# Cross-attention on one core: VectorE's mask rows, one split and one normalisation stand earlier in its order, and one set of transposes stands behind a product on TensorE

## What is computed

```python
Q = (img_embed @ Wq).reshape(B, -1, H, D).transpose(0, 2, 1, 3)
K = (sent_embed @ Wk).reshape(B, -1, H, D).transpose(0, 2, 1, 3)
V = (sent_embed @ Wv).reshape(B, -1, H, D).transpose(0, 2, 1, 3)
score = jnp.einsum('bhqd,bhkd->bhqk', Q, K) / math.sqrt(D)
score = jnp.where(mask, score, -jnp.inf)
attn = jax.nn.softmax(score, axis=-1)
ctx = jnp.einsum('bhqk,bhkd->bqhd', attn, V).reshape(B, -1, H * D)
out = ctx @ Wo + img_embed
# then layer norm over the 512 columns, times gamma, plus beta
```

## Time and profile before

| | |
|---|---|
| median of 3 runs | 364.54 us (363.69 to 364.98) |
| the profiled execution's own time | 363.32 us |
| its span, first to last instruction | 361.5 us |
| TensorE busy | 351.6 us, 97% |
| VectorE busy | 269.9 us, 75% |
| ScalarE busy | 224.4 us, 62% |
| GpSimd busy | 193.6 us, 54% |

### The profile page before, as it was taken

The page is one execution under the profiler, slowest core; times in us unless marked ns, Lnnn a source line. Parts: engine busy times, 40 slices in busy tenths (PEclk is TensorE's granted clock), DMA queues, the critical chain, the costliest instruction groups (busy, mean ns, idle before and its releaser), DMA issues. The chain is left out here.

```text
span 361.5 us, 6803 instructions
## 1 busy us (share of the span) xinstructions
PE 351.6 (97%) x2286; PEld 326.8 (90%) x2286; DVE 269.9 (75%) x504; ACT 224.4 (62%) x763; POOL 193.6 (54%) x208
## 2 busy tenths in 40 slices
PE   8999999999999899999999999999999999999993
PEld 6999999999999898899899889989988998998873
DVE  3299998773811267798897977987987988879886
ACT  2377764244334459776876776777777758767550
POOL 0045640000003856669679688688696696784234
PEclk9999999999999999999999999999999999999998
DMA  8998679866743080052241441441531422412012
GB/s 239 424 418 303 250 241 346 279 213 218 261 151 128 7 283 2 3 175 82 95 147 66 138 148 46 160 140 36 176 115 61 173 71 106 146 62 86 31 58 88
DMA packets 19682, 55.80 MB, mean 154 GB/s; under 512 B 1728, under 2 KB 3264, under 8 KB 17728
## 3 DMA queue, kind: packets, MB, share of 16 engines
q1 hardware_dynamic: 18784, 54.38, 42.2%
q10 hardware_dynamic: 864, 1.00, 1.0%
HBM read 46.98 MB, written 8.39 MB: 153 GB/s over the span
## 5 line engine op out<-in xcount | busy, mean ns | idle before, releaser
L615 PE MATMUL pair<-vw_hi,pt_hi 128*128 128x512 f32 x155 | 62.3, 402 | 0.0
L615 PE MATMUL pair<-vw_hi,pt_lo 128*128 128x512 f32 x155 | 60.8, 392 | 0.0
L615 PE MATMUL pair<-vw_lo,pt_hi 128*128 128x512 f32 x155 | 60.6, 391 | 0.0
L1182 POOL TENSOR_TENSOR out_sb<-centred,beta_sb 128x512 f32<-128x512 f32 x31 | 40.1, 1293 | 31.0 <-ACT centred L795 31.0
L750 ACT ACTIVATE prob<-c,neg_max 128x77 f32<-128x77 f32 x128 | 43.9, 346 | 0.0
L1196 POOL TENSOR_TENSOR x_sum<-xt_in 128x256 f32<-128x256 f32 x16 | 11.9, 743 | 59.5 <-DMA xt_in<-x_tiles 59.4
L1221 POOL TENSOR_TENSOR xo_lo<-x_sum,xo_hi 128x512 fp32r<-128x512 f32 x32 | 41.2, 1292 | 3.0 <-ACT xo_hi L774 3.0
L788 ACT ACTIVATE pt_hi<-pair 128x640 fp32r<-128x640 f32 x32 | 22.5, 703 | 30.4 <-PE pair L602 30.4
L1034 DVE TENSOR_TENSOR pair<-pair,x_in 128x512 f32<-128x512 f32 x31 | 21.7, 699 | 25.2 <-PE pair L615 25.1
L550 PE MATMUL pair<-a_hi,xo_hi 128*128 128x308 f32 x128 | 40.1, 313 | 0.0
L550 PE MATMUL pair<-a_lo,xo_hi 128*128 128x308 f32 x128 | 38.8, 303 | 0.0
(11 more groups left out here) (115 smaller groups left out, 958.5 us busy)
## 6 DMA issues: line engine op xcount, KB each, us to landing
w_out<-wo SPq DMA_DIRECT2D x8, 1024.0 KB, 4.8
xt_in<-x_tiles SPq DMA_DIRECT2D x16, 512.0 KB, 4.0
x_in<-x_rows SPq DMA_DIRECT2D x16, 512.0 KB, 4.8
out<-out_sb SPq DMA_DIRECT2D x31, 256.0 KB, 2.1
w_out<-wq_t SPq DMA_DIRECT2D x7, 1024.0 KB, 7.0
w_proj<-wv SPq DMA_DIRECT2D x8, 768.0 KB, 4.7
w_proj<-wk SPq DMA_DIRECT2D x6, 768.0 KB, 9.0
w_out<-wq_t SPq DMA_DIRECT2D x2, 512.0 KB, 8.2
```

Source lines behind the costliest of these rows:

```text
L615: mm = pe.matmul(ps_out[:, i % 2, 0:s.model], ps[:, j, :], v[:, b, j, :], start=(j == 0 and n == 0), stop=(j == s.key_t - 1 and n == len(p ...
L1182: pool.tensor_tensor(out_sb[i % OUT_RING][:, :], centred[i % 2][:, :], beta_sb[:, :], ALU.add)\
```

## The change

Four places in the orders of TensorE and VectorE. No instruction is added, removed or altered; only their places move (the line numbers of VectorE's instructions grow by 7, those of TensorE's later helpers by 4).

```diff
@@ TensorE: A12 becomes a helper of its own
-            def second_products(p):
+            def product_on_a(p):
 
                 b = batch_of(p)
                 pe.wait_ge(act_s1, p + 1)
                 product(p, bank_a, A12, right(a_hi, b, 1, 0), right(a_lo, b, 1, 0), False)
+
+            def second_products(p):
+
+                b = batch_of(p)
                 pe.wait_ge(act_xo_hi, SPLITS * p + 4)
@@ TensorE: pairs 0 and 1
             first_products(0)
+            product_on_a(0)
             second_products(0)
             first_products(1)
+            product_on_a(1)
             transpose_prob(0)
             second_products(1)
@@ TensorE: the loop, where the order stays as it was
                 transpose_prob(a - 1)
+                product_on_a(p)
                 second_products(p)
@@ VectorE: the last use of the first stage
                 else:
+                    if u == USES - 1:
+                        rows_for_mask()
                     split_vw(u - H)
...
-                elif u == USES - 1:
-                    rows_for_mask()
@@ VectorE: tiles 0 and 1
             residual(0)
+            split_pt(1)
             layer_norm(0)
-            split_pt(1)
@@ VectorE: the last pair
                 if p == NPAIRS - 1:
+                    normalise(a + 1)
                     split_pt(a)
-                    normalise(a + 1)
                 centre(a - 2, ps_out[:, (a - 2) % 2, 0:s.model])
```

## The result

The changed kernel takes 359.62 us (median of 4 runs, 359.38 to 359.83); the kernel before took 364.5 us in the runs beside it (363.69 to 364.98). The ratio is 0.9868 with a 95% interval of 0.9849 to 0.9887. The two profiled executions, however, stand 363.32 - 359.83 = 3.49 us apart.

What follows compares the result with a forecast made beforehand. TensorE, busy 97%, bounds the kernel, so its removed waits count: 2.1 + 0.3 + 0.5 + 0.5 = 3.4 us, off the median of 364.54 giving 361.1 us; range 359.9 to 363.2.

Steps and rivals of the forecast that it cites:

- the last line of the sum: Takes 3.4 us of removed waits off the profiled execution's time (359.9) or the median (361.1), and predicts the latter.
- Mask rows: VectorE makes them in its idle ahead of V's last split, so TensorE's bias matmul starts earlier: 2.1 us.
- The split that was overtaken: `split_vw(7)`, now behind the mask rows, still runs from 124.31 to 125.60, before transposes that come at 127.1.
- The other end, 1.9: Gain at the mask rows if VectorE is let in only when GpSimd rests: bias matmul 0.2 us late.
- Transposes behind A12: Pair 1: A12 fills TensorE's hidden wait before tile 0's transposes, saving 0.3 us.
- Split of tile 1: VectorE makes it before tile 0's layer norm, ending TensorE's stall before tile 2's transposes: counted as 0.5 us.
- the next bound: Tile 3's transposes wait for the split of tile 2, limiting the two middle places to 0.83 us together.
- The layer norm's delay: Tile 0's layer norm comes 0.74 us later, and GpSimd's work with it; GpSimd's 0.73 us idle takes it up.
- Last pair: Normalisation of tile 31 fills VectorE's idle before the split of tile 30; later waits end sooner: 0.5 us.
- the transfer: Pair 2's tiles landing late for GpSimd: gain at the mask rows eaten, 363.2 us (0.07), or slower, 365.6 (0.04).
- a new bound in the loop: Sign of being wrong: a new TensorE wait over 0.3 us, above all in pairs 0 to 3, or longer loop rounds.
- The rival of a GpSimd that holds VectorE off: Mask rows give 1.9 and the middle two places 0.5: 2.9 us in all, 361.6 us; chance 0.12.

Runs made afterwards that it cites:

- the mask rows alone: Kernel before with only the mask rows moved ahead of V's last split: 361.01 us, ratio 0.9925.
- the idle filled: Kernel before with nine matmuls on zeros run by TensorE while it waits for the unmoved mask rows: 363.18 us.
- the other three places: Changed kernel with the mask rows left where they were before: 363.2 us, ratio 0.9978 to the kernel before.
- `two_ones` early: Kernel before with only `two_ones` made ahead of V's last split, the two mask rows staying behind it: 363.03 us, ratio 0.9986.
- the transposes, the split or the last pair alone: Kernel before with one move each: tile 0's transposes behind A12, 364.49 us; tile 1's split before tile 0's layer norm, 363.69; tile 31's normalisation before tile 30's split, 363.84.

## Why the prediction was right or wrong

**The step that failed** is the last line of the sum: "Against its own time the sum gives 359.9; on the median it gives 361.1, and this is what I predict." I saw that the profiled execution was 1.2 us below the median of the runs shown and took this for an offset that the change would keep. It was no offset: the sum held every wait but left at nothing, without a reason, what may follow the longest of them, a stretch at half clock, and the change removes that too.

In these experiments the kernel before ran 69 times: 26 executions had a mean clock of 0.990 to 0.992 and a median of 364.6 us, 43 had 0.995 or more and a median of 363.3. The profiled one was of the larger group; of the three runs behind the 364.54, 364.54 and 364.98 fit the other group by their time, and 363.69 fits this one; their clocks are not known. Without the idle at the mask rows no execution was below 0.995: 10 of the changed kernel, 6 with the mask rows alone, 12 with the idle filled. With an idle of 1.8 to 2.0 us, 40 of 96 were: 26 of 69 before, 7 of 12 with the other three places, 4 of 12 with `two_ones` early, and the three executions with the transposes, the split or the last pair alone. With 4.1 us all six paid, by their times. (The count goes by the mean clock, which misses an execution like that of 364.66 us; by the times it would be 27 of 69.)

So the median's 4.9 us are some 3.6 us of waits and, for a median that falls in the lower-clock group, 1.3 us of clock. That it fell there was chance: it is the smaller group, and the median of all 69 is 363.48, 3.8 us above the changed kernel. From the larger group, 363.3 - 3.6 = 359.7, and the changed kernel takes 359.6 to 359.7; so the sum taken from the profiled execution's own time, 359.9, was the better of the two.

**Mask rows: right in kind, 0.2 us too small.** I took 2.1; the stretch gave 2.3. The part of the idle that a matmul's printed end hides was 0.27 us (2.31 - 2.04), not the 0.1 allowed. The split that was overtaken did not come late (125.37 against transposes at 126.58). GpSimd neither held VectorE off until its rest nor let it through free: 1.87 us for the three instructions instead of 1.68. The other end, 1.9, did not come.

**Transposes behind A12: right.** 0.30 forecast, 0.30 measured. Alone it is worth 0.14, since it only reaches the next stall sooner; the text gave it 0.3 because it stood beside the split.

**Split of tile 1: right.** 0.5 forecast, 0.47 measured, and with the next bound where it was said to be: the transposes of tile 3 wait 0.25 us for the split of tile 2, somewhat more than the "at most 0.2". The layer norm's delay was taken up: GpSimd's rests for pair 3 came without idle before them, and the round behind stayed at 14.10.

**Last pair: right.** 0.5 forecast, 0.51 measured, also by itself.

**The rivals.** Neither the transfer nor a new bound in the loop showed. The rival of a GpSimd that holds VectorE off was not met in the change's place, but it was real in the old one: with only `two_ones` moved away, the mask rows were held there instead, and `two_ones` took 0.79 us in place of 1.14. What it takes with GpSimd at rest is in no trace. What no rival held was a gain larger than the sum of the waits.

## What to carry to other kernels

Before adding a sum of waits to a median, ask why the profiled execution is not at that median: look at the times and the mean granted clock of each execution, and if they fall in groups, find in the profile where the clock is low, since a low clock behind the last matmul costs nothing, and whether the change touches that place. A wait of TensorE of about 2 us can cost more than its length, through a stretch at half clock behind it that one profile may not show; removing it, or filling it with matmuls on zeros, removes that too. And gains of neighbouring waits do not add by themselves: one alone gave 0.14 of its 0.3 us, since the next stall took it.

## What the runs showed of the hardware

An idle of 1.8 to 2.0 us on TensorE, after some 120 us of steady work, went with a lower mean clock in 40 of 96 executions. Three of these were profiled: the clock fell to half 0.8 to 1.1 us after work had resumed, and the stretch from pair 0 to pair 1 took 1.6 us more. Six more instructions that lengthened the idle by 2.1 us, to 4.1, lengthened all six executions by more than that, and in the profiled one the clock fell before work resumed. Why it comes in some executions and not in others was not settled.

The Trainium skill, "TensorE: Matmul & The Clock Gate", section "What's actually happening", says that the clock has only two levels, half and full; by that rule the windows of 1 us should read 0.50 or 1.00 but for those with a step in them, and they do.

VectorE's small instructions took longer beside a GpSimd instruction that reads the same memory: 1.14 us for 128 elements, and 1.37 for what takes 0.54 alone, each ending 0.15 to 0.4 us behind GpSimd's. The Trainium skill, "SBUF — State Buffer", section "SBUF: two separate sides", cited in the prediction, has an exclusive lock on a pair of ports there, and the traces agree with it. But between two GpSimd instructions that stand back to back VectorE did get its turn: three of its instructions passed between 119.87 and 121.66 while GpSimd worked on.
